# A graph network layer on one core: outward products in high and low parts, and a new order of the tail

## What is computed

```python
xn = layernorm(x)
# graph part: att is the softmax of the edge weights over the edges of one source
M    = xn @ Wm + bm                                     # 256 wide
out0 = segment_sum(att[:, None] * M[dst], src)          # A @ M
out1 = segment_sum(att[:, None] * M[src], dst)          # A.T @ M
h    = relu(layernorm(concat(out0, out1) @ W1 + b1) * gamma + beta)   # 128 wide
gnn  = where(row_sum > 0, relu(h @ W2 + b2), 0)
x1   = x + gnn + linear_attention(xn)                   # 8 heads of 64
# expert part: 8 experts, each token goes to the best one
y    = x1 + prob_max * expert[argmax](layernorm(x1))
```

## Time and profile before

| | us |
|---|---|
| median of 3 runs | 546.54 |
| lowest, highest | 544.47, 549.55 |
| the profiled execution | 546.23 |
| its span | 544.4 |
| TensorE busy, granted clock over the span | 476.6, 0.950 |
| VectorE, ScalarE, GpSimd busy | 412.8, 249.4, 198.1 |

### The profile page before, as it was taken

The page is one execution under the profiler, slowest core; times in us unless marked ns, Lnnn a source line. Parts: engine busy times, 40 slices in busy tenths (PEclk is TensorE's granted clock), DMA queues, the critical chain, the costliest instruction groups (busy, mean ns, idle before and its releaser), DMA issues.

```text
span 544.4 us, 8877 instructions
## 1 busy us (share of the span) xinstructions
PE 476.6 (88%) x2825; PEld 376.1 (69%) x2825; DVE 412.8 (76%) x792; ACT 249.4 (46%) x666; POOL 198.1 (36%) x157
## 2 busy tenths in 40 slices
PE   4289999999979999889999999799977886799992
PEld 1167878888857879676666666699855565588881
DVE  6969999999969878989999998332254758355552
ACT  0485586655751100016666666542242255456550
POOL 0078878788877778600000000000000003545422
PEclk9799999999999999999999999899998666899998
DMA  7960000000000000040000000000004951423310
GB/s 193 316 222 3 2 2 3 2 3 3 1 1 3 3 1 3 3 172 1 2 1 2 2 1 2 1 0 1 1 0 183 420 204 25 133 91 102 97 63 15
DMA packets 15776, 31.08 MB, mean 57 GB/s; under 512 B 7686, under 2 KB 8317, under 8 KB 14709
## 3 DMA queue, kind: packets, MB, share of 16 engines
q1 hardware_dynamic: 9237, 23.21, 12.5%
q0 software_dynamic: 6496, 7.31, 7.0%
HBM read 24.90 MB, written 7.38 MB: 59 GB/s over the span
## 4 chain that ended last, share of the span: by engine, by line
POOL 30%; PE 27%; DVE 23%; issue 10%; DMA 4%; ACT 3%; SPq 1%; DVEq 0%; POOLq 0%; ACTq 0%
POOL slots L448 29%; DVE s_hot L1184 8%; PE banks L818 6%; DVE d_hot L1177 5%; PE banks L526 4%; PE banks L703 4%; DVE s_one L1173 3%; PE banks L720 3%; DMA rec<-in_x 3%; PE banks L696 2%; PE banks L761 2%; PE banks L683 2%; PE banks L809 1%; DVE rec L1190 1%; PE banks L745 1%
## 5 line engine op out<-in xcount | busy, mean ns | idle before, releaser
L448 POOL DMA_INDIRECT slots<-record,row_i x118 | 160.5, 1360 | 69.0 <-issue 41.8
L459 POOL DMA_INDIRECT rec<-x_rows,get_i x17 | 20.3, 1196 | 231.8 <-DVE get_i L1335 226.9
L683 PE MATMUL banks<-d_hot,s_hot 128*128 128x251 bf16 x648 | 92.0, 276 | 5.6 <-DVE s_hot L1184 5.6
L1502 ACT ACTIVATE adj<-banks x108 | 63.7, 589 | 42.6 <-PE banks L683 42.5
L683 PEld LDWEIGHTS banks<-d_hot,s_hot 128*128 128x128 bf16 x648 | 54.4, 98 | 14.9 <-issue 6.5
L526 PE MATMUL banks<-w_hi,xT_hi 128*125 128x512 f32 (+1 forms) x160 | 59.5, 372 | 0.8 <-DVE bia L1023 0.4
L526 PE MATMUL banks<-w_hi,xT_lo 128*125 128x512 f32 (+1 forms) x160 | 58.5, 366 | 0.0
L526 PE MATMUL banks<-w_lo,xT_hi 128*125 128x512 f32 (+1 forms) x160 | 58.5, 366 | 0.0
L1184 DVE TENSOR_TENSOR s_hot<-s_one,parts 128x1024 bf16<-128x1024 bf16 (+2 forms) x87 | 51.3, 639 | 0.0
L1447 ACT ACTIVATE q_sb<-q_sb,hmax 125x64 f32<-125x64 f32 x80 | 26.7, 335 | 39.7 <-DVE hmax L1042 39.7
L526 PEld LDWEIGHTS banks<-w_hi,xT_hi 128*125 128x125 f32 x160 | 29.7, 185 | 7.1 <-issue 1.6
(11 more groups left out here) (289 smaller groups left out, 1029.5 us busy)
## 6 DMA issues: line engine op xcount, KB each, us to landing
w_raw<-in_w2f SPq DMA_DIRECT2D x4, 1024.0 KB, 8.6
w_raw<-in_wqkv SPq DMA_DIRECT2D x3, 1024.0 KB, 18.7
rec<-in_x SPq DMA_DIRECT2D x2, 1120.0 KB
x_rows<-rec SPq DMA_DIRECT2D x10, 224.0 KB
w1a<-in_w1f SPq DMA_DIRECT2D x1, 2048.0 KB, 8.7
w1b<-in_w1f SPq DMA_DIRECT2D x1, 2048.0 KB, 15.8
b_sb<-in_b2f SPq DMA_DIRECT2D x1, 2048.0 KB, 21.0
slots<-record,row_i POOLq DMA_INDIRECT x118, 2.6
```

The lines of the kernel that those rows point to most:

```text
L448: pool.indirect_dma_start(slots, bass.IndirectOffsetOnAxis(ap=row_i[:, c:c + 1], axis=0), record[:, c, :], None).then_inc(slot_st, 16)
L459: pool.indirect_dma_start(rec_c[:, c % RING, :], None, x1_rows, bass.IndirectOffsetOnAxis(ap=get_i[:, c:c + 1], axis=0)).then_inc(ld_rec[c ...
L683: mm = pe.matmul(flat_banks[:, bass.ds(at_in, AW)], s_hot[:, n % DB, i, q, :, j], d_hot[:, n % DB, q, :, j], start=False, stop=(i == WT - ...
L1502: act.activation(adj[:, bass.ds(w, BW2)], flat_banks[0:TP, bass.ds(out_at, BW2)], ACT.Copy).then_inc(win_ok, 1)
```

## The change

Columns sorted by products become 50, so GpSimd scatters 120. ScalarE takes the exponential first of all. `RUN_UP` is 18. Batches hold 4 pairs from the first, the last two hold 2; TensorE starts with the first batch. The bias additions move from the batch loop to the turn stage, one per tile.

The turned adjacency is kept in two F32R parts: ScalarE copies each of the 30 pieces to `adjT_hi`, VectorE subtracts that from the bank into `adjT_lo`. The outward columns of `msg` are split in the same way (`out_hi`, `out_lo`), once, in tiles 4 and 5. Each outward product becomes three F32R products (high-high, high-low, low-high; the low-low one is left out).

In the tail TensorE's order changes, ScalarE's with it; the centring of tiles 4 to 7 (`DA` to `DZ`) goes from VectorE to ScalarE; logits go to bank 6, and `route` has one wait less.

```diff
-PCOLS = 52
+PCOLS = 50
-PB, DB, LEAD = 4, 4, 3
+PB, DB = 4, 4
-RUN_UP = 16
+RUN_UP = 18
+DA, DZ = 4, 8
-BATCHES = [(0, 1), (1, 2), (2, 4)] + [(i, min(i + PB, PAIRS)) for i in range(4, PAIRS, PB)]
+BATCHES = [(i, i + PB) for i in range(0, PAIRS - PB, PB)] + [(PAIRS - PB, PAIRS - 2), (PAIRS - 2, PAIRS)]
...
# TensorE
-                    pe.wait_ge(batch_ok, max(n + 1, LEAD))
+                    pe.wait_ge(batch_ok, n + 1)
...
-                    m = n - 3
-                    pe.wait_ge(turn_a if m % 2 == 0 else turn_v, m // 2 + 1)
+                    pe.wait_ge(turn_v, n - 2)
...
-                    mm = pe.matmul(hid_at(w), msg[:, j, 0:GH], adjT[:, j, w * WIN:(w + 1) * WIN], start=False,
+                    cols = slice(w * WIN, (w + 1) * WIN)
+                    pe.matmul(hid_at(w), out_hi[:, j, :], adjT_hi[:, j, cols], start=False, stop=False, skip_group_check=True)
+                    pe.matmul(hid_at(w), out_hi[:, j, :], adjT_lo[w][:, j, :], start=False, stop=False, skip_group_check=True)
+                    mm = pe.matmul(hid_at(w), out_lo[:, j, 0:GH], adjT_hi[:, j, cols], start=False,
                                    stop=(j == NT - 1), skip_group_check=True)
...
+            for w in range(NW):
+                outward(w, 0)
+                if w >= 1:
+                    hid_turn(w - 1)
+                if w == NW - 1:
+                    both(x2_turn, 0)
+                outward(w, 1)
+                if w >= 2:
+                    both(hid_out, w - 2)
+                if w >= 1:
+                    hid_back(w - 1)
+            hid_turn(NW - 1)
+            both(route, 0)
+            both(x2_turn, 1)
+            both(hid_out, NW - 2)
+            hid_back(NW - 1)
+            both(route, 1)
+            both(x2_turn, 2)
+            both(hid_out, NW - 1)
+            both(route, 2)
+            both(x2_turn, 3)
+            both(route, 3)
+            both(x2_turn, 4)
+            both(route, 4)
...
# VectorE
-                if n >= 7 and n % 2 == 1 and (n - 7) // 2 < NT:
-                    t = (n - 7) // 2
-                    dve.wait_ge(mix_ok, t + 1)
-                    dve.tensor_tensor(rec[:, t, :], rec[:, t, :], bias("p"), ALU.add).then_inc(bp_ok, 1)
...
-                dve.wait_ge(turn_ps, n + 1)
-                dve.tensor_copy(adjT[:, lo:hi, t * TP:(t + 1) * TP],
-                                turn_at(n)[0:TP, 0:(hi - lo) * TP].rearrange("p (j n) -> p j n", j=hi - lo)
-                                ).then_inc(turn_v, 1)
+                dve.wait_ge(turn_a, n + 1)
+                dve.tensor_tensor(adjT_lo[t // 2][:, lo:hi, t % 2 * TP:(t % 2 + 1) * TP],
+                                  turn_at(n)[0:TP, 0:(hi - lo) * TP].rearrange("p (j n) -> p j n", j=hi - lo),
+                                  adjT_hi[:, lo:hi, t * TP:(t + 1) * TP], ALU.subtract).then_inc(turn_v, 1)
...
                 for n in range(3 * t, 3 * t + 3):
-                    if n % 2 == 1:
-                        turn_copy(n)
+                    turn_copy(n)
+                if t == 5:
+                    dve.wait_ge(out_split, 1)
+                    dve.tensor_tensor(out_lo[:, :, 0:GH], msg[:, :, 0:GH], out_hi[:, :, :], ALU.subtract).then_inc(out_split, 1)
+                dve.tensor_tensor(rec[:, t, :], rec[:, t, :], bias("p"), ALU.add).then_inc(bp_ok, 1)
...
+                if DA <= t < DZ:
+                    own_step(dve.bn_aggr(mv[:, t, :], stat[:, t, :]))
+                    dve.tensor_scalar(nmr[:, t:t + 1], mv[:, t, 0:1], -1.0, None, ALU.mult).then_inc(var2_ok, 1)
+                    return
...
# ScalarE
+            def x2_centre(t):
+                act.wait_ge(var2_ok, t + 1)
+                act.wait_ge(x2T_ps, t - 1)
+                act.activation(xn[:, t % 2, :], rec[:, t, :], ACT.Identity, bias=nmr[:, t:t + 1]).then_inc(x2_act, 1)
```

More of the change, by code:

```diff
@@ L190, in build @@
         adjw = adj[:, 0:NB * AW].rearrange("p (t w n) -> p t w n", t=NT, w=NW)
-        adjT = place("adjT", 13560, [TP, NT, N])
+        adjT_hi = place("adjT_hi", 13560, [TP, NT, N], F32R)
+        adjT_lo = [place(f"adjT_lo{w}", c, [TP, NT, WIN], F32R) for w, c in enumerate((32216, 0, 2512, 5024, 7536))]
+        out_hi = place("out_hi", 34720, [TP, NT, GH], F32R)
+        out_lo = place("out_lo", 29656, [TP, NT, MD], F32R)
         col_2 = place("col_2", 14560, [128, WIN, 2], BF16)
@@ L748, in x2_turn @@
             def x2_turn(t):
-                pe.wait_ge(x2_ok, t + 1)
+                if DA <= t < DZ:
+                    pe.wait_ge(x2_act, t - DA + 1)
+                else:
+                    pe.wait_ge(x2_ok, t + 1 if t < DA else t + 1 - (DZ - DA))
                 if t >= 2:
@@ L765, in _, with both @@
             pe.wait_ge(ld_small, 16)
[L766 to L771, removed]
-                    hid_turn(w - 1)
[L773 to L778, removed]
-                    hid_back(w - 1)
[L780 to L783, removed]
-                    route(2 * w - 5)
+            pe.wait_ge(turn_v, 3 * NT)
+            pe.wait_ge(out_split, 2)
+            def both(step, w):
+                step(2 * w)
+                step(2 * w + 1)
+            for w in range(NW):
+                outward(w, 0)
+                if w >= 1:
+                    hid_turn(w - 1)
+                if w == NW - 1:
[4 more added lines that the diff above has]
+                if w >= 1:
+                    hid_back(w - 1)
+            hid_turn(NW - 1)
[11 more added lines that the diff above has]
+            both(route, 4)
             pe.wait_ge(oh_ok, 1)
@@ L1212, in _ @@
             scale_adj(1)
+            dve.wait_ge(mix_ok, NT)
+            dve.wait_ge(row_ok, 1)
             for t in range(NT):
@@ L1377, in _ @@
         def _(act):
+            act.wait_ge(ld_w, 32)
+            act.wait_ge(top_sb, 1)
+            act.activation(record[:, :, 1], wraw[:, :], ACT.Exp, bias=top[:, 3:4]).then_inc(w_exp, 1)
             act.wait_ge(ld_x[1], 32)
@@ L1561, in _, with both @@
             act.wait_ge(ld_small, 16)
-            for w in range(1, NW + 3):
-                if w < NW + 1:
-                    hid_copy(w - 1)
-                    hid_std(w - 1)
-                    hid_relu(w - 1)
-                if 2 <= w < NW + 2:
-                    relu(2 * w - 4)
-                    relu(2 * w - 3)
-                if w >= 3:
-                    x2_copy(2 * w - 6)
-                    x2_copy(2 * w - 5)
+            def x2_centre(t):
+                act.wait_ge(var2_ok, t + 1)
+                act.wait_ge(x2T_ps, t - 1)
+                act.activation(xn[:, t % 2, :], rec[:, t, :], ACT.Identity, bias=nmr[:, t:t + 1]).then_inc(x2_act, 1)
+            def both(step, w):
+                step(2 * w)
+                step(2 * w + 1)
+            hid_copy(0)
+            for w in range(1, NW):
+                if w == NW - 1:
+                    both(x2_copy, 0)
+                hid_std(w - 1)
+                hid_copy(w)
+                if w == NW - 1:
+                    hid_relu(w - 1)
+                if w >= 2:
+                    both(relu, w - 2)
+                if w < NW - 1:
+                    hid_relu(w - 1)
+            both(x2_copy, 1)
+            hid_std(NW - 1)
+            x2_centre(4)
+            hid_relu(NW - 1)
+            x2_centre(5)
+            both(relu, NW - 2)
+            both(x2_copy, 2)
+            both(x2_centre, 3)
+            both(relu, NW - 1)
+            both(x2_copy, 3)
+            both(x2_copy, 4)
             act.wait_ge(var2_ok, NT)
```

31 lines of the change are left out of this document (15 added, 16 removed).

## The result

| | before | changed |
|---|---|---|
| median (4 runs each) | 548.04 | 523.95 |
| lowest to highest | 544.47 to 549.65 | 523.31 to 526.12 |
| ratio, 95% interval | | 0.9576 (0.9515 to 0.9637) |
| span of the profiled execution | 544.4 | 522.2 |
| its device time | 546.23 | 524.33 |

The forecast was 526.4, the range 518 to 538. The two profiled spans differ by 22.2 us. I split them at four marks: start of the first pair, start of the last pair, first outward product, and VectorE's first instruction on the logits.

The account below looks back on a forecast made before the run. Bounds: GpSimd's scatters for the first 229 us, VectorE and TensorE in the batches, TensorE in the turn stage, nothing full in the tail. 546.2 + 0.1 - 5.7 - 0.1 + 0.9 - 15.0 = 526.4 us; range 521 to 532, with rivals 1 to 3 518 to 538.

Parts of the forecast that it names:

- Tail: From the first outward product to the logits: new order and cheaper products, 53.0 us against 68.0, -15.0.
- laid out at full clock: Tail worked out from the engines' queues without clock loss: 22.9 to window 3, 23.2 to last centring, 2.8 after; 48.9 us.
- at the same 0.3 each: Tail: half clock expected in the last 15 us or so, priced at 0.3 per microsecond, +4.1 us.
- Rival 1: Tail never loses the clock, 48.9 and small change, about 49.7 us; whole kernel 523; chance 0.12.
- the cheaper product: Outward products in the tail: three one-pass products, 0.119 us each, a half 1.78 instead of 2.12; -3.4 us.
- rivals 3 and 4: Outward products: load and product not overlapping, 535 us, chance 0.05; or 0.42 us per 250-column product, 567 us, chance 0.15.
- Batches: Batch stage: without additions VectorE keeps just ahead, TensorE's pairs run 0.889 us apart; first to last pair -5.1 us.
- Start: Up to the first pair: scatters +0.1, larger first batch -0.6, extra warming zero; -0.5 us.
- buys nothing: Start: one fewer VectorE sort step (1.36 us) gains nothing, since the table waits 1.07 us for the slots.
- price without cover: Start: two more warming products (0.86 us) cost zero behind the earlier sort end; without that cover 0.9 us.
- Turn stage: Copies and subtractions: only the low part of the outward features is felt, tile 7 waits 0.7 us; +0.9 us.
- Rival 2: Tail or turn stage tighter: half clock from 25 us on (57) or subtractions at 0.8 us (+1.9); 531 us; chance 0.13.

Follow-up runs that it names:

- e4: Changed kernel with 14 warming products instead of 18: 524.31 us, ratio 0.9556 to the kernel before.
- e5: Changed kernel with 52 sorted columns and ScalarE's exponential after the statistics again, warming kept at 18: 526.75 us, ratio 0.9564 to the kernel before.
- e3: Changed kernel with the ten bias additions back in the batch loop: 526.72 us, ratio 0.9597 to the kernel before.
- e7: Changed kernel with six products of no use behind the last pair, in TensorE's wait ahead of the turn stage: 521.62 us, ratio 0.9483 to the kernel before.
- e1: Changed kernel with the old tail on three engines (order, centring on VectorE, logits in bank 1), F32R products kept: 541.64 us, ratio 0.9878 to the kernel before.
- e2: Changed kernel with outward products in float32 again, one copy per turned piece and no low parts: 526.86 us, ratio 0.9572 to the kernel before.
- e10: e9 with outward products in float32 and no low parts: 523.48 us, ratio 0.9550 to the kernel before.
- e12: e7 with outward products in float32 and one copy of each piece: 522.44 us, ratio 0.9539 to the kernel before.
- e9: Changed kernel with six products of no use ahead of the turn stage and seven in the tail's waits: 523.10 us, ratio 0.9534 to the kernel before.
- e11: Changed kernel with the high-high outward product alone, 100 of 150 products left out: 517.84 us, ratio 0.9443 to the kernel before.
- e6: Changed kernel with ScalarE's exponential after the statistics again, 50 sorted columns kept: 526.51 us, ratio 0.9579 to the kernel before.

## Why the prediction was right

The profiled execution took 524.33 us for 526.4. By stage the forecast missed by -3.3 us in the tail, +0.6 in the turn stage, +0.3 in the pairs and -0.2 up to the first pair, so the mechanism of each stage can be judged by itself.

**Tail.** The step is right and its size 3.3 us short (-18.3 for -15.0). Measured 49.8, forecast 53.0, laid out at full clock 48.9. VectorE began window 3 at 398.39, 22.9 us into the tail, as worked out, and from there its queue had no wait over 0.2 us until the last centring:

```profile
397.19 1.28 DVE L1265 TENSOR_TENSOR upd<-banks,bia 125x512 f32<-125x512 f32 x2
398.39 0.49 DVE L1244 BATCH_NORM_STATS2 stat<-banks 125x6 f32<-125x128 f32 x2
...
416.66 0.69 DVE L1271 TENSOR_TENSOR rec<-rec,upd 125x512 f32<-125x512 f32 x1 [0.19 <-ACT upd L1574]
...
420.40 0.49 DVE L1282 TENSOR_SCALAR xn<-rec,mv 125x512 f32<-125x512 f32 x1
```

That stretch took 22.5 us where 23.2 were forecast. The weight loads and stores ended as laid out: the DMA engines' share was 0.70 from 428 to 431 us and 0.07 from 431 to 434, and the first gather, at 435.02, waited for VectorE. Behind the last centring come the last transposes and the last routing, at half clock, against an earlier routing at full clock:

```profile
414.82 1.81 PE L770 MATMUL banks<-sml,x2T 128*125 128x8 f32 x16
...
420.94 1.10 PE L763 MATMUL banks<-cst,xn 125*128 125x125 f32 x4 [0.76 <-DVE xn L1282]
421.83 3.37 PE L770 MATMUL banks<-sml,x2T 128*125 128x8 f32 x16
...
425.30 0.24 DVE L1309 TENSOR_TENSOR logit<-banks,rstd 125x80 f32<-125x80 f32 x1 [1.92 <-PE banks L770]
```

The routing took 3.37 us for 1.81, and this last part 4.4 us for the 2.8 laid out. So the term that was mis-sized is the half clock of the tail, +4.1 for 15 us "at the same 0.3 each" (0.3 times 15 is 4.5; 4.1 is for 13.7 us). Measured it is about +1.6, and one price for every microsecond was the wrong form. Where VectorE is the bound, half clock on TensorE cost nothing that can be seen: with 0.5 to 7.2 us of it the stretch from window 3 to the last centring took 22.5 us in nine kernels, and with 8.5 and 8.7 us, in e4 and e5, 23.1. Behind the last centring the end waits for TensorE, and there it cost what the two routings show. The kernels with the same tail code (changed, e3 to e7) have tails of 49.7 to 52.6 us with 7.5 to 15.2 us of half clock; all but 0.6 us of that spread lies behind the last centring (4.3 to 6.5 us), where TensorE had more or less work left to do at half clock (in e7, with 5.6 us, the transposes of tile 8 were still to do, which the changed kernel had behind it). At about the 15 us that I assumed, in e5, the tail is 52.6, close to the forecast 53.0; but as 22.9 + 23.1 + 6.5, with a middle part shorter and a last part longer than laid out, so that agreement is in part luck.

Rival 1's 49.7 and its 523 us lie nearer to the measured 49.8 and 523.95 than the forecast does. Its condition, no loss of the clock, was not met (7.9 us at half), so that is no evidence for it.

**Order against products.** I gave 3.4 of the 15 us to the cheaper product. Behind the old order it is worth 0.3 (e1). Behind the new it brings window 3 forward by 2.0 us in each of three pairs (24.9 in e2, e10 and e12 for 22.9), of the 3.2 us that nine halves at 1.75 instead of 2.11 save: up to there TensorE sets most of the pace. Of these 2.0 us 0.3 to 0.4 are paid in the turn stage, and e9 and e7 lose 1.5 again behind the last centring, beside e10 and e12. In whole times it shows neither in e2 nor in e10. The spacing itself came as forecast, 0.117 for 0.119, so rivals 3 and 4 fell with it: at 250 columns a product of this type takes what its 256-column rows said. The Trainium skill's "FP8 and Floating Point Precision", "TensorE Precision Notes", counts true FP32 as four passes, one for each pairing of high and low parts. Three of these four would be an estimated 0.75 x 2.12 = 1.59 a half; the trace has 1.75, so a half came to 0.83 and not 0.75 of the old one. The load rule of the Trainium skill's "TensorE: Matmul & The Clock Gate", "LDWEIGHTS (loading the stationary operand)", is 107 ns for 128 columns; the trace has 188 ns for each of these loads (median of 50 on each of L725 to L727), so the measurement decides. Loads of 188 ns in a stream with 117 ns from product to product must overlap with their neighbours, as the forecast said, though it had them shorter.

**Batches.** -4.8 for -5.1: TensorE's pairs came 95.47/107 = 0.892 apart, with no wait for VectorE, as worked out. e3 shows the additions behind 2.9 of it; what the larger first batches give was not separated.

**Start.** The sum was right (-0.7 for -0.5), two of its steps were not. The table's wait of 1.07 us for the slots and the sort step that "buys nothing" changed places: the last scatter started 1.0 us earlier and the sort ended 1.25 us later than worked out. The sort was late because x landed later in this execution: ScalarE's first statistic starts at 22.23 for 20.74, and the sort ends nearly the same time behind that statistic in all kernels with 50 columns (see e5). So the sort was last, the table came at 233.30 and the first batch 1.2 us earlier than worked out; and the two more products for warming had lost their cover and held the first pair back 1.3 us. I had named 0.9 as the price without cover. The two misses nearly cancel, so the right sum is luck. It depends on the landing of x which of the two is last: in e2, e3, e5, e11 and e12 the sort is, as here; in e1, e4 and e6 to e10 the slots are, and there the warming ends about 1 us ahead of the first pair (2.5 in e4) and holds nothing back. Whether the 1.3 us can be had back where the sort is last is open, since the profiled execution of e4 is of the other kind.

**Turn stage.** +1.4 for +0.8. TensorE waited for VectorE once, at tile 7, where it was laid out, two tiles behind the subtraction for `out_lo`:

```profile
365.87 1.41 PE L700 MATMUL banks<-cst,adj 125*125 125x125 f32 x10 [0.30 <-DVE adjT_lo L1220]
```

From these transposes to those before (362.20) it is 3.67 us instead of 3.21, so the wait cost 0.46 where 0.7 was laid out. The split costs 0.3 to 0.4 at equal clock (e5 against e2, e9 against e10), less than the 0.9 forecast. The rest of the 1.4 is half clock, 6.8 us for 3.4, which I had left as it was before: e5, with 3.4, is only 0.2 us above the kernel before.

**Rival 2**, half clock from 25 us on or subtractions of 0.8 us, was not met: the clock first fell 35 us into the tail, and the subtractions took 0.67 us (median). Nor was its 531.

## What to carry to other kernels

Find the queue whose next instruction waits while independent work stands behind it. Here a new tail, with the routing of two tiles moved behind the outward products, gave 12 us by itself and about 6 more through the clock, together 17.9 of the 22.2 us between the two profiled executions (that the moved routing is the main part of it is my reading of the waits in the earlier trace rows and e1; apart from 1.3 us of centring the parts were not separated). Rewriting the products gave 2.0 us where TensorE was still the bound, and almost none of it reached the end. Where a stage starts with a wait of TensorE of about 3 us, as here, a few products of no use in exactly that wait are worth trying; in e9, in small waits near the end, they stood in the way. Ask of half clock where it falls: in a stretch that another engine bounds it cost nothing here, and in the last few microseconds, where all waited for TensorE, it set the end. And compare variants stage by stage, with the stages that the edit does not touch as a measure of chance: they differ by up to 4.1 us here.

## What the runs showed that I had not expected

The same tail code ran in 49.7 to 52.6 us, with half-clock stretches that began at different places. What moves them is not shown: one kernel varies too (three executions of e5 took 526.6 to 527.4 us and one 522.67). So a gain in one stage can seem paid back in another: e7 gained 2.8 us in the turn stage, and its tail was 1.2 us longer, with 10.5 us of half clock for 7.9. And in the profiled execution of e4 a gap of 2.5 us ahead of the first pair cost 2.5 us behind it, while that of 1.38 us in the kernel before cost nothing that the clock shows.
